# Attention queries and keys in three stacked copies: one rounded similarity pass of 96 rows in place of an exact one of 32

## The chip, the cores and the metric

The kernel runs on one core of a Trainium2 chip. The metric is the device time of one execution in microseconds (us). The kernel before was timed three times: 608.33, 611.28 and 616.86 us, median 611.28. One more execution was recorded by the hardware profiler; the rows below come from it.

Engines are named as in the profile: PE is TensorE (matmul), DVE is VectorE, ACT is ScalarE, POOL is GpSimd, SP is SyncE.

## The reference

An image batch of 16 x 16 x 16 x 192 goes through three layers with residuals: a blockwise DCT convolution, a gated attention over the 256 tokens of each image, and a mixture of 8 experts with two chosen per token. Only the attention's queries and keys matter here:

```python
def _L1_attn_ref(x, ln_w, ln_b, W_hidden, b_hidden, W_qk, b_qk, gamma, beta, W_out, b_out):
    normed = _layernorm(x, ln_w, ln_b)
    hg = jax.nn.silu(jnp.einsum('bsd,hd->bsh', normed, W_hidden) + b_hidden)
    v, gate = jnp.split(hg, 2, axis=-1)
    Z = jax.nn.silu(jnp.einsum('bsd,qd->bsq', normed, W_qk) + b_qk)   # 32 wide
    q = Z * gamma[0] + beta[0]
    k = Z * gamma[1] + beta[1]
    sim = jnp.einsum('bid,bjd->bij', q, k) / seq_len
    A = jnp.square(jax.nn.relu(sim))
    V = jnp.einsum('bij,bjd->bid', A, v) * gate
    out = jnp.einsum('bih,dh->bid', V, W_out) + b_out
    return out + x
```

## The kernel before, in words

The program has three stages, each a software pipeline written out by hand per engine: the convolution over 16 images (to about 120 us), the attention over 16 images (to about 300 us), and the experts' tiles. Every engine runs its own `attn_step(i)` for i from -1 to 16; in step i it works on image i, on the front of image i+1 and on the tail of image r = i-1. The order within an engine is the order of the code; engines meet through semaphores.

**Rounded and exact products.** A product with operands of type `fp32r` takes one pass of PE and rounds its operands. Where the kernel wants more precision it splits an operand into a rounded high part and the low rest and adds several such passes (`products`, five passes). A product with plain `f32` operands is exact and appears in the trace as two matmul rows for one call.

**PE, step i.** The v products of image i (10 matmuls of 392 columns), then the wait for `qk_done` and the similarity (`ps_sim`, two calls, one per half of the keys), the gate products (15 matmuls), the transposes of image i+1, `attend` (which waits for `attn_done` and `l1_done`), two small matmuls that count rows per expert, the z product of image i+1 (`z_product`, five matmuls), the output product. The next step's v products follow.

**ACT, step i.** silu of v, relu and square of the similarity, silu of the gate, the rounded copies of the next image's transposed rows (`nB_bias`, `n_hi`), silu of z into `zT` (L843), `normalise` for image i+2, tanh, and the expert rows of image r (`row_a`, L854).

**DVE, step i.** `finish_tokens(r)` (residual, moments, variance `u_var`), `logits_of_base`, `logits_of_tokens`, `choose(r)`, `low_parts(i+1)` (L940, L941), the gating product (L1253), `scale_tokens(r)` (L1189 to L1196), `query_key(i+1)` (L1063), `count(r)` (L1090 to L1092) and `place(r)` (L1100 to L1106). `scale_tokens` waits for POOL's power `u_pow`; `place` ends with the routing weights, on `weights_done`.

**POOL, step i.** `u_pow(r)` (L649, waits for DVE's `u_var`), the bias add on image i's residual (L654), two id updates (L661), the copy of `row_a` into `row_b` (L663, waits for ACT's row_a), then the wait for `weights_done` and `slots_done` of DVE's `place(r)`, and four indirect DMAs that scatter the rows to the experts' lists (L672). The next step's `u_pow` stands behind these four.

`query_key(i)` is two DVE instructions, each 32 partitions by 256:

```python
for n, dst in enumerate((qT, kT)):
    last = dve.tensor_scalar(dst[:, :], zT[:, :], gb_sb[:, n:n + 1], gb_sb[:, 2 + n:3 + n], ALU.mult, ALU.add)
last.then_inc(qk_done, 1)
```

In step 0 DVE also computes the layer-norm scales of the last four images, right behind `query_key(1)`; `logits_of_base(1)`, which gives `l1_done`, comes after them. `chain.link(ins)` makes DVE wait for its own instruction `ins` to finish before the next one.

Of the kernel before, what the change touches and what calls it, by code (L numbers as in the profile page):

```python
# [24 lines left out]
SEQ = SIDE * SIDE  # L25
P = 128
# [9 lines left out]
HID = 2 * D  # L36
QK = 32
EXPERTS, FF = 8, 768
FCHUNKS = FF // P
# [156 lines left out]
def build(nc, x, consts, w1, b1, ln_w, ln_b, w_hid, w_qk, b_hid, b_qk, b_i, gamma, beta, w_out, w_out_t, b_out, b_col, w_r,  # L196
# [8 lines left out]
    with ctx:  # L205
# [36 lines left out]

        w_qk_sb = sb("w_qk_sb", [P, 2, QK])
        w_qk_hi = sb("w_qk_hi", [P, 2, QK], f32r)
        w_qk_lo = sb("w_qk_lo", [P, 2, QK], f32r)
        w_out_sb = sb("w_out_sb", [P, HID // P, OUT_W])
# [3 lines left out]
        ln_sb = sb("ln_sb", [P, 2, 2])  # L250
        gb_sb = sb("gb_sb", [QK, 4])
        b_out_sb = sb("b_out_sb", [P, D])
# [14 lines left out]

        zT, qT, kT = (xc[0:QK, :, :, :].rearrange("p a t c -> p (a t c)")[:, n * SEQ:(n + 1) * SEQ] for n in range(3))
        hT = sb("hT", [P, 2, FCHUNKS, TWO])
# [102 lines left out]
        ps_nT = ps[:, 0, :].rearrange("p (k n) -> p k n", k=2)  # L372
        ps_z = ps[0:QK, 1, 0:SEQ]
        ps_sim = ps[:, 1, :].rearrange("p (t n) -> p t n", t=HALVES)
# [109 lines left out]
        def over_channels(ap):  # L484

            return ap.unsqueeze(1).unsqueeze(3).broadcast_to((P, HALVES, GROUPS, GC))

        def pad_lists(eng, experts, done):
# [216 lines left out]
        def _(act):  # L705
# [24 lines left out]
            def bias_high_parts():  # L730

                act.wait_ge(parts_done, 1)
                act.wait_ge(prep_ps, 1)
                hi, lo = slice(BIAS_HI, BIAS_HI + 1), slice(BIAS_LO, BIAS_LO + 1)
                act.activation(w_lo[hi, 1, 0:HID], ps_b_hid[hi, :], ACT.Copy)
                act.activation(b_hi[lo, 0:HID].bitcast(f32r), ps_b_hid[lo, :], ACT.Copy)
                act.activation(w_qk_lo[hi, 1, :], ps_b_qk[hi, :], ACT.Copy)
                act.activation(b_qk_hi[lo, :].bitcast(f32r), ps_b_qk[lo, :], ACT.Copy).then_inc(bias_hi_done, 1)
# [139 lines left out]
        def _(dve):  # L878
# [38 lines left out]
            def bias_low_parts():  # L917
# [4 lines left out]
                dve.tensor_tensor(w_lo[lo, 1, 0:HID], ps_b_hid[lo, :], b_hi[lo, 0:HID], ALU.subtract)  # L922
                dve.tensor_tensor(w_qk_lo[lo, 1, :], ps_b_qk[lo, :], b_qk_hi[lo, :], ALU.subtract)
                for row in (hi, lo):
# [135 lines left out]
            def query_key(i):  # L1060
                dve.wait_ge(z_done, i + 1)
                for n, dst in enumerate((qT, kT)):
                    last = dve.tensor_scalar(dst[:, :], zT[:, :], gb_sb[:, n:n + 1], gb_sb[:, 2 + n:3 + n],  # L1063
                                             ALU.mult, ALU.add)
                last.then_inc(qk_done, 1)
# [213 lines left out]
            dve.wait_ge(ld_rest, 16)  # L1279
            pipeline(dve, attn_step, **ATTN, chain=chain, per=8)  # L1280

# [39 lines left out]
        def _(pe):  # L1321
# [36 lines left out]
            def prepare():  # L1358
# [4 lines left out]
                folded_bias(ps_b_hid, hid_in[:, :, 0:HID], b_hid_sb[:, 0:HID])  # L1363
                folded_bias(ps_b_qk, w_qk_sb, b_qk_sb)
                for k in range(NKC):
# [73 lines left out]
            def z_product(i):  # L1439
                pe.wait_ge(nT_done, i + 1)  # L1440
                pe.wait_ge(nB_bias_done, i + 1)
                products(ps_z, w_qk_hi, w_qk_lo, slice(0, QK), False).then_inc(z_ps, 1)

# [53 lines left out]
            def attn_step(i):  # L1497
# [6 lines left out]
                if not absent(i):  # L1504

                    pe.wait_ge(qk_done, i + 1)
                    for t in range(HALVES):
                        last = mm(ps_sim[:, t, :], kT[:, t * P:(t + 1) * P], qT[:, :])
                    last.then_inc(sim_ps, 1)
# [121 lines left out]
```

## Time and profile before

| what | value |
|---|---|
| median of three runs | 611.28 us (608.33 to 616.86) |
| profiled execution, its own time | 614.02 us |
| its span, first to last instruction | 612.3 us |
| mean granted TensorE clock | 0.981 |
| PE busy | 578.3 us, 94% |
| DVE busy | 394.4 us, 64% |
| ACT busy | 332.1 us, 54% |
| POOL busy | 266.4 us, 44% |
| chain that ended last | PE 71%, DVE 10%, DMA 7%, issue 6% |

The shares are averages over the three stages. What matters is the attention stage, from about 120 to 300 us: there a view by stretches, a view in order of time and the chain that ended last are read together. In a row of the time view the first number is the start, the second the time from the first start to the last end of the instructions merged in the row (the count is at the end), and in brackets stands how long the engine sat idle before and what released it.

### The profile page before, as it was taken

Reading aid. Unit: us, or ns where it says so; the run is one execution under the profiler, and the core shown is the slowest. Engines: PE = TensorE matmul, PEld = TensorE weight load, DVE = VectorE, ACT = ScalarE, POOL = GpSimd, SP = SyncE. Lnnn points to the kernel's source line nnn. Section 1 sums busy time; section 2 is a strip of 40 time slices with the busy share of each in tenths; the row PEclk is TensorE's granted clock in tenths of the full one; section 3 lists DMA queues with packets and bytes.
Section 4 is the critical chain, followed back from the end, with each engine's and each line's share of the span. In section 5 each row is a group of like instructions: output and inputs, shape, how many; then the busy total and the mean of one; then the engine's idle time right before and its main releaser. Section 6 shows DMA issues by size and latency. Waiting matters only on the chain.

```text
span 612.3 us, 14343 instructions
## 1 busy us (share of the span) xinstructions
PE 578.3 (94%) x3844; PEld 544.6 (89%) x3845; DVE 394.4 (64%) x1516; ACT 332.1 (54%) x722; POOL 266.4 (44%) x314
## 2 busy tenths in 40 slices
PE   3999999898999999999898999999999999999992
PEld 2899888887888888888797999999999999999992
DVE  4568888757777767778876555555555555555650
ACT  1433233465666676666673555555555555556650
POOL 3313322103656565565565444444444444444432
PEclk9979999998999999999998999999999999999997
DMA  8980000310111111112224333333333333333221
GB/s 241 412 332 1 0 0 2 126 49 33 60 52 65 39 68 48 59 59 79 66 87 85 50 45 50 52 48 50 52 51 48 50 52 52 45 39 40 41 27 20
DMA packets 31832, 42.45 MB, mean 69 GB/s; under 512 B 4596, under 2 KB 27797, under 8 KB 31670
## 3 DMA queue, kind: packets, MB, share of 16 engines
q0 software_dynamic: 13488, 13.74, 14.4%
q1 hardware_dynamic: 18196, 28.16, 14.1%
q8 instruction: 15, 0.25, 0.2%
q14 instruction: 19, 0.16, 0.1%
q10 hardware_dynamic: 114, 0.15, 0.1%
HBM read 24.46 MB, written 17.57 MB: 69 GB/s over the span
## 4 chain that ended last, share of the span: by engine, by line
PE 71%; DVE 10%; DMA 7%; issue 6%; POOL 2%; DVEq 2%; ACT 1%; POOLq 0%; SPq 0%; ACTq 0%
PE ps L1326 68%; DMA out_rows<-const,y_id 6%; PE ps L1330 2%; PE ps L1331 2%; DMA X<-in_x 1%; DVEq L988 1%; POOL xn L639 1%; DVE newton L969 1%; POOL y_id L688 1%; DVE gsq L1005 1%; DVE mom L990 0%; DVE newton L1000 0%; DVE newton L1010 0%; DVE newton L994 0%; DVE newton L1009 0%
## 5 line engine op out<-in xcount | busy, mean ns | idle before, releaser
L806 ACT ACTIVATE hT<-ps,b_i_sb 128x256 f32<-128x256 f32 (+1 forms) x240 | 94.5, 448 | 114.3 <-PE ps L1326 114.2
L1326 PE MATMUL ps<-w_o_sb,hT 128*128 x852 | 146.9, 329 | 0.9 <-DVE const L1308 0.9
L1326 PEld LDWEIGHTS ps<-w_o_sb,hT 128*128 128x128 f32 x852 | 139.1, 192 | 1.5 <-issue 1.5
L692 POOL DMA_INDIRECT out_rows<-const,y_id x71 | 115.7, 1630 | 41.9 <-POOL y_id L688 29.4
L1326 PE MATMUL ps<-n_hi,we_hi 128*128 128x256 f32 (+1 forms) x468 | 124.7, 289 | 0.0
L1326 PE MATMUL ps<-n_hi,we_lo 128*128 128x256 f32 (+1 forms) x468 | 92.9, 280 | 0.0
L1211 DVE TENSOR_TENSOR we_lo<-we_all,we_hi 128x768 fp32r<-128x768 f32 x80 | 75.3, 982 | 23.1 <-issue 23.0
L1326 PEld LDWEIGHTS ps<-n_hi,we_hi 128*128 128x128 f32 x468 | 88.9, 190 | 0.0
L1326 PEld LDWEIGHTS ps<-n_hi,we_lo 128*128 128x128 f32 x468 | 71.6, 189 | 0.0
L1326 PE MATMUL ps<-nA_lo,we_hi 128*128 128x256 f32 (+1 forms) x234 | 65.6, 280 | 0.0
L787 ACT ACTIVATE we_hi<-we_all 128x768 fp32r x80 | 63.5, 849 | 3.4 <-DVE tile_expert L1149 2.6
L1308 DVE TENSOR_TENSOR const<-ps,b_o_sb 128x384 f32<-128x384 f32 (+1 forms) x40 | 20.5, 513 | 69.4 <-DMA out_rows<-const,y_id 56.3
L688 POOL TENSOR_TENSOR y_id<-y_row,no_offset 128x2 int32<-128x2 int32 (+1 forms) x40 | 9.8, 246 | 116.0 <-DVE const L1314 90.7
L1326 PE MATMUL ps<-attnT,hT 128*128 128x256 f32 x192 | 45.9, 391 | 2.3 <-issue 2.3
L1326 PEld LDWEIGHTS ps<-nA_lo,we_hi 128*128 128x128 f32 x234 | 44.3, 189 | 0.0
L672 POOL DMA_INDIRECT lists<-row_a,slots x32 | 32.8, 1026 | 22.8 <-POOL row_b L663 11.6
L639 POOL TENSOR_TENSOR xn<-xc,grs 128x384 f32<-128x384 f32 x16 | 13.8, 865 | 66.4 <-DVE grs L1011 54.5
L1326 PEld LDWEIGHTS ps<-attnT,hT 128*128 128x128 f32 x192 | 36.3, 196 | 7.0 <-issue 2.5
L1326 PE MATMUL ps<-w_out_sb,hT 128*128 128x200 f32 x192 | 36.6, 341 | 2.9 <-DVE hT L1253 2.6
L1326 PE MATMUL ps<-conv_only,coef 96*108 96x192 f32 x192 | 38.9, 356 | 0.4
L1326 PEld LDWEIGHTS ps<-w_out_sb,hT 128*128 128x128 f32 x192 | 31.8, 190 | 6.3 <-issue 3.9
L1221 DVE TENSOR_TENSOR nA_lo<-ps,n_hi 128x256 fp32r<-128x256 f32 (+1 forms) x39 | 15.3, 393 | 33.1 <-ACT n_hi L796 33.0
(238 smaller groups left out, 1154.1 us busy)
## 6 DMA issues: line engine op xcount, KB each, us to landing
we_all<-in_w_i SPq DMA_DIRECT2D x8, 768.0 KB, 13.7
conv_only<-lists SPq DMA_DIRECT2D x31, 194.0 KB, 2.8
w_o_sb<-in_w_o SPq DMA_DIRECT2D x8, 576.0 KB, 17.9
out_rows<-X SPq DMA_DIRECT2D x16, 192.0 KB
X<-in_x SPq DMA_DIRECT2D x1, 1536.0 KB, 11.7
out_rows<-const,y_id POOLq DMA_INDIRECT x71, 3.6
conv_only<-lists SPq DMA_DIRECT2D x9, 97.0 KB, 2.3
we_all<-in_w_hid SPq DMA_DIRECT2D x1, 776.0 KB, 8.0
```

Source lines behind the costliest of these rows:

```text
L639: pool.tensor_tensor(grouped(xn[:, :, :]), grouped(xc[:, odd, :, :]), over_channels(grs[:, :]), ALU.mult).then_inc(xn_done, 1)
L672: pool.indirect_dma_start(out=lists, out_offset=bass.IndirectOffsetOnAxis(ap=slots[:, c, t:t + 1], axis=0), in_=rows[:, t, :], in_offset=N ...
L688: pool.tensor_tensor(y_id[:, odd, 0:n], y_row[:, odd, 0:n], no_offset[:, 0:n], ALU.add).then_inc(id_done[odd], 1)
L692: pool.indirect_dma_start(out=out, out_offset=bass.IndirectOffsetOnAxis(ap=y_id[:, odd, t:t + 1], axis=0), in_=y_sb[:, odd, t, :], in_offs ...
L787: act.activation(we_hi[:, odd, here].unsqueeze(1), we_all[:, ds(e, 1), here], ACT.Copy).then_inc(we_hi_done, 1)
L806: last = act.activation(hT[:, odd, f, 0:n].unsqueeze(1), ps_h[:, b, c, 0:n].unsqueeze(1), ACT.Gelu, bias=b_i_sb[:, ds(e * FCHUNKS + f, 1)])
L1211: last = dve.tensor_tensor(we_lo[:, odd, here].unsqueeze(1), we_all[:, ds(e, 1), here], we_hi[:, odd, here].bitcast(f32).unsqueeze(1), ALU ...
L1221: dve.tensor_tensor(lo[:, 0:n * P], turned[:, 0, 0:n * P], hi[:, 0:n * P].bitcast(f32), ALU.subtract)
L1308: dve.tensor_tensor(here, ps_y[:, 0:n, :], b_o_sb[:, ds(e, 1), :].broadcast_to((P, n, D)), ALU.add).then_inc(y_read, 1)
L1326: return pe.matmul(dst, lhsT, rhs, start=start, stop=stop)
L1330: pe.transpose(dst[:, 0, here], rows[:, 0:KA], K("ident"))
L1331: return pe.transpose(dst[:, 1, here], rows[:, KA:WIDE], K("ident"))
```

## The change

z, the input of the queries and keys, is computed three times in one projection: the weights, gamma and beta are repeated three times over, so that z stands in 96 partitions. From it DVE makes `q_parts` and `k_parts`, 96 partitions by 256 of type `fp32r`: rounded values in all three blocks, and then in one block each (rows 64 to 95 for the queries, 32 to 63 for the keys) the exact value minus the rounded one. One rounded pass over 96 rows then sums high x high, high x low and low x high. For the subtraction the exact values of that block are computed as well, into `q_full` and `k_full`.

`query_key` has six instructions in place of two, with a wait of DVE for its own fourth before the fifth. The similarity is a rounded product in place of an exact one. The chain's count per step goes from 8 to 9.

```diff
+QK3 = 3 * QK
...
-        w_qk_sb = sb("w_qk_sb", [P, 2, QK])
-        w_qk_hi = sb("w_qk_hi", [P, 2, QK], f32r)
-        w_qk_lo = sb("w_qk_lo", [P, 2, QK], f32r)
+        w_qk_sb = sb("w_qk_sb", [P, 2, QK3])
+        w_qk_hi = sb("w_qk_hi", [P, 2, QK3], f32r)
+        w_qk_lo = sb("w_qk_lo", [P, 2, QK3], f32r)
...
-        gb_sb = sb("gb_sb", [QK, 4])
+        gb_sb = sb("gb_sb", [QK3, 4])
...
-        zT, qT, kT = (xc[0:QK, :, :, :].rearrange("p a t c -> p (a t c)")[:, n * SEQ:(n + 1) * SEQ] for n in range(3))
+        zT, q_full, k_full = (xc[0:QK3, :, :, :].rearrange("p a t c -> p (a t c)")[:, n * SEQ:(n + 1) * SEQ]
+                              for n in range(3))
+
+        q_parts = sb("q_parts", [QK3, SEQ], f32r)
+        k_parts = sb("k_parts", [QK3, SEQ], f32r)
...
-        ps_z = ps[0:QK, 1, 0:SEQ]
+        ps_z = ps[0:QK3, 1, 0:SEQ]
...
-                act.activation(w_qk_lo[hi, 1, :], ps_b_qk[hi, :], ACT.Copy)
+                act.activation(three_times(w_qk_lo[hi, 1, :]), one_for_three(ps_b_qk[hi, :]), ACT.Copy)
...
-                dve.tensor_tensor(w_qk_lo[lo, 1, :], ps_b_qk[lo, :], b_qk_hi[lo, :], ALU.subtract)
+                dve.tensor_tensor(three_times(w_qk_lo[lo, 1, :]), one_for_three(ps_b_qk[lo, :]),
+                                  one_for_three(b_qk_hi[lo, :]), ALU.subtract)
...
             def query_key(i):
                 dve.wait_ge(z_done, i + 1)
-                for n, dst in enumerate((qT, kT)):
-                    last = dve.tensor_scalar(dst[:, :], zT[:, :], gb_sb[:, n:n + 1], gb_sb[:, 2 + n:3 + n],
-                                             ALU.mult, ALU.add)
+                scales = [(gb_sb[:, n:n + 1], gb_sb[:, 2 + n:3 + n]) for n in range(2)]
+                rows = (slice(2 * QK, QK3), slice(QK, 2 * QK))
+                for full, here, (by, plus) in zip((q_full, k_full), rows, scales):
+                    dve.tensor_scalar(full[here, :], zT[here, :], by[here, :], plus[here, :], ALU.mult, ALU.add)
+                for parts, (by, plus) in zip((q_parts, k_parts), scales):
+                    last = dve.tensor_scalar(parts[:, :], zT[:, :], by, plus, ALU.mult, ALU.add)
+                chain.link(last)
+                for parts, full, here in zip((q_parts, k_parts), (q_full, k_full), rows):
+                    last = dve.tensor_tensor(parts[here, :], full[here, :], parts[here, :].bitcast(f32), ALU.subtract)
                 last.then_inc(qk_done, 1)
...
-            pipeline(dve, attn_step, **ATTN, chain=chain, per=8)
+            pipeline(dve, attn_step, **ATTN, chain=chain, per=9)
...
-                products(ps_z, w_qk_hi, w_qk_lo, slice(0, QK), False).then_inc(z_ps, 1)
+                products(ps_z, w_qk_hi, w_qk_lo, slice(0, QK3), False).then_inc(z_ps, 1)
...
-                        last = mm(ps_sim[:, t, :], kT[:, t * P:(t + 1) * P], qT[:, :])
+                        last = mm(ps_sim[:, t, :], k_parts[:, t * P:(t + 1) * P], q_parts[:, :])
...
-    w_qk = np.ascontiguousarray(two_parts(L1_attn_W_qk).swapaxes(0, 1))
+    w_qk = np.ascontiguousarray(np.tile(two_parts(L1_attn_W_qk).swapaxes(0, 1), (1, 1, 3)))
```

Two places show how the instructions stand. The first is DVE's stretch from `scale_tokens` to `place` in the attention loop, before (xc holds zT, qT and kT; list_at and slot belong to `count`):

```order
L1196 TENSOR_TENSOR diff<-diff,u_scale 128x2
L1063 TENSOR_SCALAR xc<-xc,gb_sb 32x256 [waits z_done]
L1063 TENSOR_SCALAR xc<-xc,gb_sb 32x256
L1090 TENSOR_TENSOR slot<-list_at,ps 128x8 [waits prefix_ps]
L1091 TENSOR_TENSOR slot<-slot,in_first 128x8 [waits dve_self]
L1092 TENSOR_TENSOR list_at<-list_at,ps 128x8
L1100 TENSOR_TENSOR picked<-chosen,slot 128x32 [waits prefix_read,ld_const]
L1102 TENSOR_REDUCE slots<-picked 128x4 [waits dve_self]
```

Two instructions make queries and keys, and `count` follows them. The same stretch in the changed kernel (xc now holds zT, q_full and k_full):

```order
L1216 TENSOR_TENSOR diff<-diff,u_scale 128x2
L1079 TENSOR_SCALAR xc<-xc,gb_sb 32x256 [waits z_done]
L1079 TENSOR_SCALAR xc<-xc,gb_sb 32x256
L1081 TENSOR_SCALAR q_parts<-xc,gb_sb 96x256
L1081 TENSOR_SCALAR k_parts<-xc,gb_sb 96x256
L1084 TENSOR_TENSOR q_parts<-xc,q_parts 32x256 [waits dve_self]
L1084 TENSOR_TENSOR k_parts<-xc,k_parts 32x256
L1110 TENSOR_TENSOR slot<-list_at,ps 128x8 [waits prefix_ps]
L1111 TENSOR_TENSOR slot<-slot,in_first 128x8 [waits dve_self]
L1112 TENSOR_TENSOR list_at<-list_at,ps 128x8
L1120 TENSOR_TENSOR picked<-chosen,slot 128x32 [waits prefix_read,ld_const]
L1122 TENSOR_REDUCE slots<-picked 128x4 [waits dve_self]
```

Four more instructions stand between `scale_tokens` and `count`, one of them with a wait for DVE itself; nothing else is moved.

The second place is PE's similarity, between the last v products (392 columns) and the first gate products, before:

```order
L1326 MATMUL ps<-w_lo,nB_bias 128x392
L1326 MATMUL ps<-w_lo,n_hi 128x392
L1326 MATMUL ps<-xc 128x256 x2
L1326 MATMUL ps<-n_hi,w_hi 128x256
L1326 MATMUL ps<-nA_lo,w_hi 128x256
```

The two calls read qT and kT in xc, exact products. The same place in the changed kernel:

```order
L1346 MATMUL ps<-w_lo,nB_bias 128x392
L1346 MATMUL ps<-w_lo,n_hi 128x392
L1346 MATMUL ps<-q_parts,k_parts 128x256 x2
L1346 MATMUL ps<-n_hi,w_hi 128x256
L1346 MATMUL ps<-nA_lo,w_hi 128x256
```

The two calls keep their place and their shape and read the rounded parts; the order of PE is otherwise the same.

## Rows read from the trace of the kernel before

**Rows 1.** Busy time per stretch: window, length, PE, PEld, DVE, ACT, POOL, PEclk, DMA.
```profile
114.00:120.00 6.00, 4.50 (x27) 4.26 (x28) 4.19 (x16) 3.36 (x8) 0.00 (x0) 1.00 0.41 115
...
138.00:144.00 6.00, 3.72 (x13) 2.92 (x11) 4.77 (x26) 2.25 (x5) 2.02 (x4) 0.78 0.09 33
...
190.00:201.00 11.00, 11.00 (x67) 9.72 (x67) 8.31 (x43) 7.62 (x18) 6.44 (x9) 1.00 0.15 54
```

**Rows 2.** The chain that ended last, in order of time: one step of the attention.
```profile
196.12 10.30 PE ps L1326 x60
```

**Rows 3.** Time view of POOL in the attention (columns as told above).
```profile
150.36 1.23 POOL L672 DMA_INDIRECT lists<-row_a,slots  x1 [1.13 <-issue]
...
193.16 1.06 POOL L672 DMA_INDIRECT lists<-row_a,slots  x1 [0.97 <-POOL row_b L663]
...
198.04 0.73 POOL L649 TENSOR_TENSOR u_pow<-u_var,minus_half 128x2 f32<-128x2 f32 x1
198.74 0.99 POOL L654 TENSOR_TENSOR X<-X,b_out_sb 128x384 f32 x1
...
203.88 1.05 POOL L672 DMA_INDIRECT lists<-row_a,slots  x1 [0.97 <-POOL row_b L663]
...
289.63 1.05 POOL L672 DMA_INDIRECT lists<-row_a,slots  x1 [1.00 <-DVE row_b L1106]
```

**Rows 4.** Time view of DVE in the same step.
```profile
197.31 0.42 DVE L940 TENSOR_TENSOR nA_lo<-ps,n_hi 128x256 fp32r<-128x256 f32 x1 [1.32 <-ACT n_hi L838]
197.75 0.43 DVE L941 TENSOR_TENSOR n_hi<-ps,n_hi 64x256 fp32r<-64x256 f32 x1
...
199.14 0.62 DVE L1189 TENSOR_TENSOR newton<-u_neg,u_pow 128x2 f32<-128x2 f32 x1
...
200.26 0.15 DVE L1196 TENSOR_TENSOR diff<-diff,u_scale 128x2 f32<-128x2 f32 x1
200.33 0.72 DVE L1063 TENSOR_SCALAR xc<-xc,gb_sb 32x256 f32<-32x256 f32 x2
200.98 0.14 DVE L1090 TENSOR_TENSOR slot<-list_at,ps 128x8 f32<-128x8 f32 x1
...
201.99 0.16 DVE L1106 TENSOR_SCALAR row_b<-tanh_d 128x2 f32<-128x2 f32 x1
```

**Rows 5.** Time view of PE: z product (two of five), similarity, first gate product.
```profile
198.60 0.28 PE L1326 MATMUL ps<-n_hi,w_qk_hi 128*32 128x256 f32 x1
198.72 0.28 PE L1326 MATMUL ps<-nA_lo,w_qk_hi 128*32 128x256 f32 x1
...
203.31 1.13 PE L1326 MATMUL ps<-xc 32*128 32x256 f32 x4
204.36 0.39 PE L1326 MATMUL ps<-n_hi,w_hi 128*128 128x256 f32 x1
```

**Rows 6.** Time view of DVE and POOL in the last image, where POOL waits for DVE.
```profile
314.05 0.50 POOL L663 COPY row_b<-row_a 128x384 f32<-128x384 f32 x1 [1.64 <-ACT row_a L854]
314.05 0.54 DVE L1100 TENSOR_TENSOR picked<-chosen,slot 128x32 f32<-128x32 f32 x1
...
314.80 0.16 DVE L1106 TENSOR_SCALAR row_b<-tanh_d 128x2 f32<-128x2 f32 x1
315.88 1.05 POOL L672 DMA_INDIRECT lists<-row_a,slots  x1 [1.33 <-DVE row_b L1106]
```

**Rows 7.** One line, shortest, median and longest duration in ns: DVE L1314, per-partition scalars.
```profile
L1314 DVE TENSOR_SCALAR const<-const,meta x71: 310/320/322, 316.0 to 602.6; 128x192 f32<-128x192 f32 x71
```

**Rows 8.** Time view of DVE and PE in images 0 and 1.
```profile
123.01 0.72 DVE L1063 TENSOR_SCALAR xc<-xc,gb_sb 32x256 f32<-32x256 f32 x2
123.87 1.13 PE L1326 MATMUL ps<-xc 32*128 32x256 f32 x4
...
131.06 0.72 DVE L1063 TENSOR_SCALAR xc<-xc,gb_sb 32x256 f32<-32x256 f32 x2 [0.45 <-ACT xc L843]
...
140.50 4.52 PE L1326 MATMUL ps<-attnT,hT 128*128 128x256 f32 x12 [2.28 <-issue]
```

More of the change, by code:

```diff
@@ L486, in over_channels, with three_times, one_for_three @@
             return ap.unsqueeze(1).unsqueeze(3).broadcast_to((P, HALVES, GROUPS, GC))
+        def three_times(ap):
+            return ap.rearrange("p (n c) -> p n c", n=3)
+        def one_for_three(ap):
+            return ap.unsqueeze(1).broadcast_to((1, 3, QK))
         def pad_lists(eng, experts, done):
@@ L1363, in prepare @@
                 folded_bias(ps_b_hid, hid_in[:, :, 0:HID], b_hid_sb[:, 0:HID])
-                folded_bias(ps_b_qk, w_qk_sb, b_qk_sb)
+                folded_bias(ps_b_qk, w_qk_sb[:, :, 0:QK], b_qk_sb)
                 for k in range(NKC):
@@ L1612 @@
         "b_qk": np.asarray(L1_attn_b_qk).reshape(1, -1), "b_i": np.ascontiguousarray(b_i.T),
-        "gamma": np.ascontiguousarray(np.asarray(L1_attn_gamma).T),
-        "beta": np.ascontiguousarray(np.asarray(L1_attn_beta).T),
+        "gamma": np.ascontiguousarray(np.tile(np.asarray(L1_attn_gamma).T, (3, 1))),
+        "beta": np.ascontiguousarray(np.tile(np.asarray(L1_attn_beta).T, (3, 1))),
         "w_out": packed(L1_attn_W_out, P), "w_out_t": packed(np.asarray(L1_attn_W_out).T, KC),
```

## The prediction

> **What bounds the kernel now.** I read the busy time per stretch first. In the attention's steady state PE is busy in 11.00 of 11.00 us, DVE in 8.31, ACT in 7.62, POOL in 6.44, at a granted clock of 1.00 [rows 1]. The chain that ended last agrees: through ten steps it shows PE pieces of 10.30 us [rows 2], and nothing else of weight. So this stage is bound by PE, with a step of 203.88 - 193.16 = 10.72 us by POOL's first scatter [rows 3]; the 13 steps from 150.36 to 289.63 give 139.27 / 13 = 10.71.
>
> The change shortens work on PE and lengthens work on DVE, so the next question is how much room DVE has. Busy time says 2.7 us in 11, but DVE does not work alone: there is a ring through DVE and POOL. POOL's four scatters of one image wait for the weights that DVE's `place` writes; POOL's `u_pow` of the next image stands behind these four; DVE's `scale_tokens` waits for `u_pow`; behind it come `query_key`, `count`, `place`, and with these the next scatters. The time view gives each link:
>
> - first scatter to `u_pow`: 198.04 - 193.16 = 4.88 [rows 3];
> - `u_pow` start to the end of DVE's first Newton step: 199.14 + 0.62 = 199.76, so 1.72 [rows 3, 4]. That step is stretched until POOL's bias add ends, 198.74 + 0.99 = 199.73;
> - Newton end to `query_key`: 200.33 - 199.76 = 0.57 [rows 4];
> - `query_key` to `count`: 200.98 - 200.33 = 0.65 [rows 4];
> - `count` to the end of `place`: 201.99 + 0.16 - 200.98 = 1.17 [rows 4];
> - end of `place` to the first scatter, where POOL really waits for it: 315.88 - (314.80 + 0.16) = 0.92 [rows 6].
>
> The ring is 9.91 us long, against a step of 10.72. It has only 0.81 us of room, and in the row of 203.88 POOL's bracket names the copy of row_b and not DVE as the last to come [rows 3], as it must where the ring is slack.
>
> **The change part by part.**
>
> The similarity on PE. Two exact calls are four matmul rows and last from 203.31 to the first gate product at 204.36, so 1.05 us [rows 5]. Rounded passes of 256 columns start 0.12 apart (198.60, 198.72); two take 0.24. PE gains 0.8 us per image, and a step bound by PE would be 9.92.
>
> The z product. Five passes of 256 columns stay five passes of 256 columns; only the stationary side is 96 wide and not 32. I take nothing for it; whatever it were, PE's idle time below would hide it. ACT's silu of z works on 96 partitions and 256 elements as before: nothing.
>
> `query_key` on DVE. Before, the two instructions take 0.72 together and `count` starts 0.65 after the first [rows 4]: one starts about 0.325 after the other and lasts 0.395. Now there are six. What their order costs is bounded from both sides.
>
> The lower end: all overlap as the two do now. The fourth starts at 0.975 and ends at 1.37; DVE's wait for itself adds about 0.04; two subtractions of 256 elements follow 0.34 apart; `count` starts at 2.09. That is 2.09 - 0.65 = 1.44 more.
>
> The upper end: instructions that change the block of partitions do not overlap. L941 works on partitions 64 to 127, L940 before it on all, and it starts at 197.75, 0.02 after the 0.42 of L940 have ended (197.31 + 0.42), while the pair of `query_key` overlaps by 0.07 [rows 4]. The six work from partitions 64, 32, 0, 0, 64, 32, and `count` from 0. Then the first starts 0.10 later than now, the next two at 0.41 and 0.82, the fourth at 1.15, ending at 1.54; the subtractions of 0.42 each run from 1.58 and 2.02 to 2.44; `count` starts at 2.46. That is 0.10 + 2.46 - 0.65 = 1.91 more.
>
> The Trainium skill has a rule for this, in "VectorE: DVE Perf Modes", section "Two Vector instructions with no wait between them": an instruction whose input or output starts in another quadrant of 32 partitions than the one before it starts only when every earlier one has finished. By it the added time is the 1.91, without it the 1.44. L941's row agrees with it.
>
> On top of this a subtraction with both inputs in SBUF can meet POOL's copy of row_b, which lasts 0.50. In the last image such an instruction (`picked`) and the copy both start at 314.05; it takes 0.54 and ends 0.04 after the copy [rows 6]. The Newton step in rows 4 does the same with the bias add. So this costs between 0 and 0.5; I take 0.1, since the copy can start only after tanh and row_a, which follow `scale_tokens`, and so should be nearly over when the subtractions come. The scaling instructions take per-partition scalars, as L1314 does, and L1314 is never stretched in 71 cases, though POOL issues its indirect DMAs in the same stage [rows 7]; for them I take no wait. The skill's page "SBUF — State Buffer", section "Who interferes with whom", says the same: a VectorE instruction with two SBUF inputs and a GpSimd one that reads SBUF exclude each other for their whole length.
>
> I take 1.91 + 0.1 = 2.0 per image (ends 1.4 and 2.4). Behind the last subtraction stand `count` and `place`, on which POOL's scatters wait, so all of it lies in the ring: 9.91 + 2.0 = 11.9 us per step (11.3 to 12.3). That is longer than the PE step of 9.92, so PE's gain is idle time (DVE's own work, 8.31 x 10.72 / 11 + 2.0 = 10.1, also stays below it), and the step grows by 11.9 - 10.7 = 1.2 us (0.6 to 1.6). From the first scatter to the fourteenth there are 13 such steps: 15.6 us (8 to 21).
>
> Before the steady state. In image 0, `query_key` starts at 123.01 and PE's similarity follows at 123.87 [rows 8]. The queries are now ready at 123.01 + 2.44 = 125.45, PE starts about 1.7 later and saves 0.8: +0.9. In image 1, `query_key` at 131.06 stands ahead of the layer-norm scales, on which `l1_done` and with it PE's `attend` at 140.50 wait, idle 2.28 [rows 8]: 1.8 more (no earlier instruction to wait out). In image 2 the ring closes for the first time; its first scatter at 150.36 is not bound by DVE yet, and of the 2.0 I count 0.6. Together 3.3 (2.2 to 3.9).
>
> After the fourteenth scatter no `query_key` is left; the last images' chain runs through DVE's weight parts and POOL, shifted as a whole. The experts' stage is the same code. The wider weights cost three ACT and three DVE instructions with up to 64 more elements each per part, 0.1 us or less each by the 0.42 for 256 [rows 4], in the first two conv steps: 0.2, at most 0.5.
>
> Sum: 15.6 + 3.3 + 0.2 = 19.1 us. Against the profiled execution's 614.02 (1.7 of it outside the span) that is 633.1; this execution lies 2.7 above the median of 611.28, so the forecast for a median is 611.28 + 19.1, rounded to 630. The ends give 622 and 637.
>
> **The rivals.**
>
> *The six overlap after all* (0.13). The block of partitions does not matter to instructions that read SBUF only, and the copy is not met. For: L941 reads PSUM too, so its row is not quite the same case. Against: in the same rows every pair that stays on one block of partitions overlaps, and only L941 does not. The ring is 9.91 + 1.44 = 11.35, 0.63 more per step: 8.2, with 2.2 at the start and 0.2, 622.
>
> *PE stays the bound and the kernel gets faster* (0.06). The ring would have to have room that I don't see: the 0.92 from `place` to the scatter would have to pass while DVE still works, as a fixed time of POOL's after its copy and not after the last release. For: behind the copy POOL takes 0.97 as well [rows 3]. Against: in rows 6 the scatter keeps 0.92 from DVE's end while the copy had ended at 314.55, 1.33 before. It decides if the ring with the new `query_key` stays under 9.92; then 14 images save 0.8: 611.28 - 11 = 600.
>
> *PE's clock falls* (0.11). With 2.0 us of idle time per step of 11.9 PE might be granted less. For: after the idle 2.28 the clock is 0.78 in 138 to 144 [rows 1, 8]. Against: from 114 to 120 PE is busy in only 4.50 of 6.00 us, at a clock of 1.00 [rows 1]. PE's 9.92 would pass 11.9 at a clock below 0.83; at 0.78 it is 12.7, 0.8 more per step, about 11 in 13 steps: 641.
>
> **How the numbers follow.** The forecast, the ring with about 2.0 us more in it, has 0.70; its own range is 624 to 637. The point is its 630. The rivals have 0.13 (622), 0.06 (600) and 0.11 (641). The range from 618 to 640 holds nearly all of the forecast, the first rival and part of the clock's, and leaves out the faster case. Two per cent, about what a measurement of this kernel can tell from no change, is 12.2 us: 599.1 and 623.5. Slower than that: 0.67 of the forecast, the clock's 0.11, and 0.03 of the first rival, 0.81. Within: 0.03, 0.10 and half of the faster case's, 0.16. Faster: 0.03.
>
> **What would show it.** The interval between first scatters should be 11.9 and the bracket of the first one should name DVE's row_b of `place`, not POOL's copy. From the first `query_key` instruction to `count` it should be about 2.5, with no overlap between the instructions that start on different partitions, and one of the subtractions may be stretched by POOL's copy. PE should sit idle ahead of the similarity, released by DVE, and be busy in about 10 of 12 us. Two similarity rows per image should stand 0.12 apart. The forecast is wrong if PE stays busy throughout with steps near 9.9, if `query_key` takes under 2.0, or if POOL's scatters are released by its copy as before.

## The result, and the profile after

The changed kernel takes 636.19 us (median of four runs, 635.88 to 637.79) against 610.53 for the kernel before in the same comparison (four runs, 608.33 to 616.86). The ratio is 1.0403, interval 1.0356 to 1.0451: slower by 4%. The profiled execution of the changed kernel took 635.88 us with a span of 634.2, the one before 614.02 with 612.3; the spans differ by 21.9.

Busy time per stretch, after, in the order window, length, PE, PEld, DVE, ACT, POOL, PEclk, DMA; this answers to [rows 1]:

```profile
138.00:144.00 6.00, 3.00 (x7) 2.49 (x8) 4.82 (x28) 0.07 (x1) 2.00 (x4) 0.56 0.09 33
...
202.00:214.00 12.00, 10.16 (x62) 9.17 (x62) 10.31 (x47) 7.31 (x17) 6.43 (x9) 1.00 0.16 56
```

In the steady state PE now idles 1.84 of 12 us, at a clock of 1.00, and DVE does 10.31; but DVE isn't full either. No engine is the bound; a chain is. POOL's time view shows it:

```profile
152.19 1.23 POOL L685 DMA_INDIRECT lists<-row_a,slots  x1 [1.83 <-issue]
...
209.39 0.51 POOL L676 COPY row_b<-row_a 128x384 f32<-128x384 f32 x1 [1.87 <-ACT row_a L867]
212.73 1.05 POOL L685 DMA_INDIRECT lists<-row_a,slots  x1 [2.84 <-DVE row_b L1126]
...
217.60 0.74 POOL L662 TENSOR_TENSOR u_pow<-u_var,minus_half 128x2 f32<-128x2 f32 x1
...
224.79 1.06 POOL L685 DMA_INDIRECT lists<-row_a,slots  x1 [2.84 <-DVE row_b L1126]
...
285.03 1.05 POOL L685 DMA_INDIRECT lists<-row_a,slots  x1 [2.73 <-DVE row_b L1126]
...
310.87 1.05 POOL L685 DMA_INDIRECT lists<-row_a,slots  x1 [2.73 <-DVE row_b L1126]
```

The step is 224.79 - 212.73 = 12.06 (before 10.72 in [rows 3]). The bracket of the first scatter has changed: it was 0.97 behind POOL's copy, now it is 2.84, and the releaser is DVE's row_b. POOL sits with its copy done and waits for `place`.

DVE in the same step, the answer to [rows 4]:

```profile
207.96 0.82 DVE L1079 TENSOR_SCALAR xc<-xc,gb_sb 32x256 f32<-32x256 f32 x2
208.80 0.41 DVE L1081 TENSOR_SCALAR q_parts<-xc,gb_sb 96x256 fp32r<-96x256 f32 x1
209.13 0.40 DVE L1081 TENSOR_SCALAR k_parts<-xc,gb_sb 96x256 fp32r<-96x256 f32 x1
209.57 0.60 DVE L1084 TENSOR_TENSOR q_parts<-xc,q_parts 32x256 fp32r<-32x256 f32 x1
210.18 0.41 DVE L1084 TENSOR_TENSOR k_parts<-xc,k_parts 32x256 fp32r<-32x256 f32 x1
210.63 0.16 DVE L1110 TENSOR_TENSOR slot<-list_at,ps 128x8 f32<-128x8 f32 x1
...
211.67 0.16 DVE L1126 TENSOR_SCALAR row_b<-tanh_d 128x2 f32<-128x2 f32 x1
...
213.36 0.39 DVE L1181 TENSOR_SCALAR u_neg<-mom 128x2 f32<-128x2 f32 x1
...
214.02 0.37 DVE L1193 SCALAR_TENSOR_TENSOR from_base<-ps,a_scale,sums 128x8 f32<-128x8 f32 x2 [0.26 <-DVE both_parts L1184]
...
218.44 0.89 DVE L1209 TENSOR_TENSOR newton<-u_neg,u_pow 128x2 f32<-128x2 f32 x1 [0.65 <-POOL u_pow L662]
...
220.02 0.82 DVE L1079 TENSOR_SCALAR xc<-xc,gb_sb 32x256 f32<-32x256 f32 x2
```

Follow the ring from the scatter at 212.73: `u_pow` 4.87 later; end of the Newton step at 219.33, 1.73 later; next `query_key` at 220.02, 0.69; `query_key` to `count`, 210.63 - 207.96 = 2.67; to the end of `place`, 211.83, 1.20; to the scatter, 0.90. The sum is 12.06, which is the step.

PE, the answer to [rows 5] and [rows 8] (image 1, a steady step, and step 13, behind DVE's first counting of tiles):

```profile
141.00 5.09 PE L1346 MATMUL ps<-attnT,hT 128*128 128x256 f32 x12 [4.96 <-issue]
...
210.65 0.50 PE L1346 MATMUL ps<-q_parts,k_parts 96*128 96x256 f32 x2 [0.41 <-DVE k_parts L1084]
210.99 0.28 PE L1346 MATMUL ps<-n_hi,w_hi 128*128 128x256 f32 x1
...
214.49 1.75 PE L1346 MATMUL ps<-attnT,hT 128*128 128x256 f32 x7 [1.12 <-issue]
...
287.93 4.47 PE L1346 MATMUL ps<-attnT,hT 128*128 128x256 f32 x12 [2.15 <-issue]
```

The similarity has shrunk as the change intends: the first gate product follows 0.34 behind it, where it was 1.05. But PE waits 0.41 for the queries and then 1.12 ahead of `attend`.

Where the 21.9 us of span went, by POOL's first scatters:

| stretch | before | after | difference |
|---|---|---|---|
| to image 0's `query_key` | 123.01 | 120.63 | -2.4 |
| from there to the first scatter | 27.35 | 31.56 | +4.2 |
| next 11 steps | 118.03 | 132.84 | +14.8 |
| two steps after these | 21.24 | 25.84 | +4.6 |
| 14th to 15th first scatter | 15.46 | 14.22 | -1.2 |
| from the 15th to the end | 307.2 | 309.1 | +1.9 |

The first line lies ahead of what the change touches in the attention. In the twelve profiled executions here image 0's `query_key` starts between 117.55 and 123.01, latest in the one of the kernel before; its granted clock in 30 to 60 us is 0.85, that of the changed kernel 0.95.

### The profile page after: what moved, and what is told of

It is laid out like the page before. It is cut to its first block, busy times and chain, and to the rows that moved or that the text cites. A ratio compares the mean times of both kernels' runs of the same rounds, so it can differ in the third digit from the quotient of the medians.

```text
span 634.2 us, 14353 instructions
## 1 busy us (share of the span) xinstructions
PE 569.7 (90%) x3812; PEld 540.7 (85%) x3813; DVE 426.6 (67%) x1580; ACT 333.8 (53%) x722; POOL 273.2 (43%) x314
## 4 chain that ended last, share of the span: by engine, by line
PE 46%; DVE 2%; issue 1%; DMA 1%; POOLq 0%; DVEq 0%; ACT 0%; ACTq 0%; POOL 0%
PE ps L1346 44%; PE ps L1350 1%; PE ps L1351 1%; DMA out_rows<-const,y_id 1%; POOLq L206 0%; DVE const L1334 0%; DVE hT L1273 0%; DVE we_lo L1231 0%; DVE meta L1244 0%; DVE const L1328 0%; DVE over L1138 0%; DVE nA_lo L1241 0%; DVE n_tiles L1140 0%; DVE n_hi L1242 0%; ACTq L796 0%
## 5 line engine op out<-in xcount | busy, mean ns | idle before, releaser
L705 POOL DMA_INDIRECT out_rows<-const,y_id x71 | 123.2, 1736 | 41.9 <-POOL y_id L701 29.4
L1231 DVE TENSOR_TENSOR we_lo<-we_all,we_hi 128x768 fp32r<-128x768 f32 x80 | 73.4, 959 | 22.1 <-issue 20.6
L1346 PE MATMUL ps<-attnT,hT 128*128 128x256 f32 x192 | 49.0, 409 | 21.9 <-issue 21.9
L1346 PEld LDWEIGHTS ps<-attnT,hT 128*128 128x128 f32 x192 | 37.7, 203 | 30.0 <-issue 24.9
L1346 PE MATMUL ps<-w_out_sb,hT 128*128 128x200 f32 x192 | 38.2, 351 | 4.1 <-DVE hT L1273 4.0
L1346 PEld LDWEIGHTS ps<-w_out_sb,hT 128*128 128x128 f32 x192 | 33.5, 197 | 5.8 <-issue 4.3
L1346 PE MATMUL ps<-conv_only,coef 96*108 96x192 f32 x192 | 37.4, 346 | 0.4
```

Source lines behind the costliest of these rows:

```text
L705: pool.indirect_dma_start(out=out, out_offset=bass.IndirectOffsetOnAxis(ap=y_id[:, odd, t:t + 1], axis=0), in_=y_sb[:, odd, t, :], in_offs ...
L1231: last = dve.tensor_tensor(we_lo[:, odd, here].unsqueeze(1), we_all[:, ds(e, 1), here], we_hi[:, odd, here].bitcast(f32).unsqueeze(1), ALU ...
L1346: return pe.matmul(dst, lhsT, rhs, start=start, stop=stop)
```

## The experiments

The kernels are named by what was done. Ratios are against the kernel before, run beside them (611.48, 611.45 or 610.96 us). A step is the mean interval of POOL's first scatters over eight or nine steady steps.

**Late `place` alone.** The kernel before, similarity and queries untouched, with four instructions of the change's shapes behind `qk_done` whose output nobody reads:

```diff
                 last.then_inc(qk_done, 1)
...
+                for n, here in enumerate(rows):
+                    last = dve.tensor_scalar(full_any[here, :], z_any[here, :], ...)
+                chain.link(last)
+                for here in rows:
+                    dve.tensor_tensor(parts_any[here, :], full_any[here, :], z_any[here, :], ALU.subtract)
```

> The kernel before with its exact similarity; qk_done is given by the second of the two query instructions as before, and behind them DVE runs four more that nobody reads (two scalings of 32 rows from partitions 64 and 32, DVE's wait for itself, two subtractions of 32 rows). The ring theory (POOL's scatters wait for DVE's place, which now comes about 2.0 us later): step between first scatters 12.0, POOL's first scatter released by DVE's row_b, about 634 us. The rival (the changed kernel is slower because PE's similarity waits for its queries): the queries are on time here, so steps stay at 10.7 and the time at 611.

Measured: 630.28 us, ratio 1.031 (1.0276 to 1.0345), step 12.02. In the time views of POOL and PE:

```profile
207.33 1.13 PE L1337 MATMUL ps<-xc 32*128 32x256 f32 x4
...
209.83 1.05 POOL L676 DMA_INDIRECT lists<-row_a,slots  x1 [2.82 <-DVE row_b L1117]
```

PE's similarity starts without a wait, and the step is still 12.02, with the same bracket on the scatter. So delaying `count` and `place` is by itself enough for the step of the changed kernel; late queries aren't needed for it. The other 6 us of the changed kernel are not in this one: of the 5.4 by which its span is shorter, 2.4 lie ahead of the first scatter and 1.8 in the two steps behind the steady ones.

**Rounded values only.** The changed kernel without its exact values and subtractions. All three blocks then hold rounded values and high x high is summed three times, so the output is not only less exact, as the expectation has it, but another one; the kernel serves for its time:

```diff
-                for full, here, (by, plus) in zip((q_full, k_full), rows, scales):
-                    dve.tensor_scalar(full[here, :], zT[here, :], by[here, :], plus[here, :], ALU.mult, ALU.add)
...
-                chain.link(last)
-                for parts, full, here in zip((q_parts, k_parts), (q_full, k_full), rows):
-                    last = dve.tensor_tensor(parts[here, :], full[here, :], parts[here, :].bitcast(f32), ALU.subtract)
...
```

> The changed kernel without the low parts: the exact values and the two subtractions are left out, so query_key is two instructions of 96 rows as short as before (the output is less exact). Ring theory: the ring is 9.9 again and PE's step is 10.7 less 0.8, so steps of 9.9 to 10.0, about 601 us (597 to 605). Rival (the wider z product or the rounded similarity cost something): steps at 10.7 or more, 611 or more.

Measured: 604.41 us, ratio 0.9893 (0.9844 to 0.9942), step 10.19. This is 1% less than the kernel before, and the interval lies wholly below 1: it is the gain on PE that the change could have had. Other tokens may go to other experts here, but from the last first scatter to the end the profile has 296.7 us, against 296.4 before, so the gain isn't from there. The run shows the ring once more:

```profile
204.60 0.51 POOL L676 COPY row_b<-row_a 128x384 f32<-128x384 f32 x1 [1.81 <-ACT row_a L867]
204.70 0.44 DVE L1121 TENSOR_SCALAR row_a<-tanh_d 128x2 f32<-128x2 f32 x1
206.11 1.06 POOL L685 DMA_INDIRECT lists<-row_a,slots  x1 [1.00 <-DVE row_b L1121]
```

With a faster PE the scatter is released by DVE and no longer by the copy. `place`'s first weight takes 0.44 where it takes 0.16 elsewhere, and ends 0.03 after POOL's copy; the second starts at 205.05. The old ring of 9.91 plus about 0.27 is the step.

**No copy on POOL.** ACT writes row_b too:

```diff
-                    pool.tensor_copy(row_b[:, :, DATA:ROW], row_a[:, :, DATA:ROW]).then_inc(row_b_done, 1)
...
-                    pool.wait_ge(row_b_done, r + 1)
...
-                    for t in range(HALVES):
...
+                    for rows in (row_a, row_b):
+                        for t in range(HALVES):
...
```

> The changed kernel without POOL's copy of the expert rows: ACT writes row_b itself, by two more instructions behind row_a. In the changed kernel the first subtraction of query_key takes 0.60 and ends 0.27 after POOL's copy, the second 0.41. Theory (the subtraction waits for the copy's end): it takes 0.42, the six instructions and count come closer by 0.18, the step falls from 12.07 to 11.89 and the time by 13 x 0.18 = 2.3 to about 634. Rival (the 0.60 is DVE's wait for its own fourth instruction): the subtraction stays at 0.60 and the step at 12.07, 636.

Measured: 632.33 us, ratio 1.0348 (1.024 to 1.0456), step 11.84.

**One block of partitions.** The same, and the exact values made over all 96 partitions:

```diff
-                for full, here, (by, plus) in zip((q_full, k_full), rows, scales):
-                    dve.tensor_scalar(full[here, :], zT[here, :], by[here, :], plus[here, :], ALU.mult, ALU.add)
+                for full, (by, plus) in zip((q_full, k_full), scales):
+                    dve.tensor_scalar(full[:, :], zT[:, :], by, plus, ALU.mult, ALU.add)
```

> The kernel without POOL's copy, and the exact values made over all 96 partitions from partition 0, not over 32 partitions from 64 and from 32: the first four instructions of query_key now start on one partition. Theory (an instruction that starts on another block of partitions waits for the end of the one before): the four start 0.33 apart, where the changed kernel shows 0.41, 0.42 and 0.33, and the first of them need not wait out scale_tokens (0.1); so about 0.28 less from scale_tokens to count, a step of about 11.6 and a time of about 630. Rival (no such wait; the 0.41 is the length of an instruction that works on 32 partitions): 96 partitions change nothing, step as without the copy alone, about 11.9, 634.

Measured: 628.6 us, ratio 1.0257 (1.0169 to 1.0345), step 11.53. DVE without the copy:

```profile
204.16 0.15 DVE L1215 TENSOR_TENSOR diff<-diff,u_scale 128x2 f32<-128x2 f32 x1
204.35 0.82 DVE L1078 TENSOR_SCALAR xc<-xc,gb_sb 32x256 f32<-32x256 f32 x2
...
205.95 0.42 DVE L1083 TENSOR_TENSOR q_parts<-xc,q_parts 32x256 fp32r<-32x256 f32 x1
```

and with one block of partitions:

```profile
204.52 0.15 DVE L1215 TENSOR_TENSOR diff<-diff,u_scale 128x2 f32<-128x2 f32 x1
204.59 0.73 DVE L1078 TENSOR_SCALAR xc<-xc,gb_sb 96x256 f32<-96x256 f32 x2
...
206.01 0.42 DVE L1083 TENSOR_TENSOR q_parts<-xc,q_parts 32x256 fp32r<-32x256 f32 x1
```

Without POOL's copy the first subtraction falls from 0.60 to 0.42: the 0.18 was the copy. With one block the first instruction follows `diff` by 0.07 and not 0.19, and from it to the subtraction 1.42 pass and not 1.60, though each instruction now works on three times the partitions. So the step loses 0.12 + 0.18 = 0.30 (measured 11.84 - 11.53 = 0.31). An instruction that changes the block of partitions waits for the one before, which is what the Trainium skill states in "VectorE: DVE Perf Modes", section "Two Vector instructions with no wait between them"; here the wait costs 0.08 to 0.12 a time.

**`place` first.** The changed kernel with `count` and `place` ahead of `query_key`:

```diff
+                if not absent(r):
+                    count(r)
+                    place(r)
                 if not absent(i + 1):
                     query_key(i + 1)
...
-                if not absent(r):
-                    count(r)
-                    place(r)
```

> The changed kernel with count and place ahead of query_key in DVE's order; nothing else. Ring theory: the six instructions are out of the ring, which is 9.3; DVE's own order of work (newton, count and place, six query instructions, residual to choose, low parts, gating) is then the longest at about 10.5 a step; about 614 us (608 to 619). Rival (late queries hold PE): the queries come 1.2 us later still, so the steps stay at 12 or grow to 13, 636 or more.

Measured: 628.05 us, ratio 1.027 (1.0221 to 1.0319), step 11.26. A miss. PE, ACT, DVE and POOL in one step:

```profile
201.48 2.83 PE L1346 MATMUL ps<-attnT,hT 128*128 128x256 f32 x12
...
205.33 1.64 ACT L729 ACTIVATE normed<-X,n_bias,n_scale 128x192 f32 x4
206.87 0.19 ACT L862 ACTIVATE tanh_d<-diff 128x2 f32<-128x2 f32 x1
...
207.09 0.17 DVE L1126 TENSOR_SCALAR row_a<-tanh_d 128x2 f32<-128x2 f32 x1 [0.57 <-ACT tanh_d L862]
...
208.07 0.50 POOL L676 COPY row_b<-row_a 128x384 f32<-128x384 f32 x1 [2.90 <-ACT row_a L867]
208.20 0.52 DVE L1081 TENSOR_SCALAR q_parts<-xc,gb_sb 96x256 fp32r<-96x256 f32 x1
```

`place` now meets tanh, which stands on ACT behind `normalise`, which stands behind the silu of z. In the kernel before this wait was covered by `query_key` itself. A new loop closes: PE's `attend` and z, ACT's silu, `normalise` and tanh, DVE's `place` and `query_key`, and the next `attend`, at 212.74, one step of 11.26 later. `low_parts` is no link of it: it ends at 203.73, and z starts at 204.20, right behind `attend` and the two small counting matmuls.

**`place` first, exact values on ACT.** As above, and ACT computes the two exact values behind `row_a`; the subtractions wait for them:

```diff
+                if not absent(i + 1):
+                    act.wait_ge(z_done, i + 2)
+                    for n, (full, at) in enumerate(((q_full, 2 * QK), (k_full, QK))):
+                        here = slice(at, at + QK)
+                        last = act.activation(full[here, :], zT[here, :], ACT.Identity, ...)
+                    last.then_inc(exact_done, 1)
...
-                for full, here, (by, plus) in zip((q_full, k_full), rows, scales):
-                    dve.tensor_scalar(full[here, :], zT[here, :], by[here, :], plus[here, :], ALU.mult, ALU.add)
...
+                dve.wait_ge(exact_done, i + 1)
```

> The changed kernel with place ahead of query_key and the two exact values computed by ACT behind row_a in place of DVE; same result. Ring theory: DVE's order of work is 0.85 shorter than in e2_place_first, about 9.7, PE 9.9 and the ring through row_a and its copy about 10.0; steps of 10.0, about 602 us (598 to 608), faster than the kernel before. Rival (ACT's extra 0.7 us delays silu of v or tanh): steps of 10.5 or more, 609 or more.

Measured: 634.92 us, ratio 1.0367 (1.033 to 1.0403), step 11.38. The second miss, of the same cause: behind `normalise`, tanh and `row_a` the exact values are late.

```profile
202.49 0.42 DVE L1091 TENSOR_TENSOR q_parts<-xc,q_parts 32x256 fp32r<-32x256 f32 x1 [1.31 <-ACT xc L875]
```

The 0.82 saved on DVE comes back as a wait of 1.31.

**`normalise` ahead of z.** `place` first, and ACT runs `normalise(i+2)` before the silu of z, so that tanh isn't behind it:

```diff
+                if not absent(i + 2):
+                    normalise(i + 2)
                 if not absent(i + 1):
                     act.wait_ge(z_ps, i + 2)
                     act.activation(zT[:, :], ps_z, ACT.Silu).then_inc(z_done, 1)
-                if not absent(i + 2):
-                    normalise(i + 2)
```

> The changed kernel with count and place ahead of query_key on DVE, and with ACT's normalise of image i+2 ahead of its silu of z, so that tanh and row_a no longer stand behind normalise. Theory (with place first the step of 11.26 is DVE's own order, 10.5 of work and 0.57 of waiting for tanh): the wait is gone, the step is about 10.7, DVE is busy all but 0.3 of it, and the time is about 7 below that of place first alone, 621. Rival 1 (the ring through row_a and the copy binds, 11.24): row_a starts 1.3 earlier, so the step falls as well, but with POOL's copy and not DVE's row_b ahead of the first scatter, and DVE idle more. Rival 2 (normalise ahead of z delays z, and with it queries and similarity): step stays near 11.2, 628.

Measured: 631.81 us, ratio 1.0302 (1.0215 to 1.0388), step 12.03. The wait for tanh is gone, yet the step has grown. DVE and POOL:

```profile
204.34 0.73 POOL L662 TENSOR_TENSOR u_pow<-u_var,minus_half 128x2 f32<-128x2 f32 x1
204.44 1.63 DVE L1105 TENSOR_TENSOR in_first<-chosen 128x8 f32<-128x8 f32 x1
205.04 0.99 POOL L667 TENSOR_TENSOR X<-X,b_out_sb 128x384 f32 x1
```

`in_first` adds two tiles of 128x8 and takes 0.15 in the changed kernel. Here it takes 1.63 (the median of its 16 executions is 1.62) and ends 0.04 after POOL's bias add.

**The same, with a later bias add.** One wait more on POOL:

```diff
+                    if not absent(i + 1):
+                        wait(pool, nT_done, i + 2)
                     wait_alone(pool, sum_done, i + 1, ld_const)
                     pool.tensor_tensor(whole, whole, b_out_sb[:, :]...
```

> The kernel with normalise ahead of z and place first, with one wait more: POOL's bias add waits until DVE's low_parts of the next image is done. In the kernel without this wait DVE's in_first (two inputs in SBUF, 0.15 elsewhere) takes 1.63 and ends with POOL's bias add in every step, and the step is 12.03 where 10.7 was expected. Theory (that instruction waits for the POOL instructions that began just after it was due): in_first takes 0.15 to 0.9 (u_pow alone may still meet it), the step falls by 0.8 to 1.4 to 10.6 to 11.2, the time to 614 to 621. Rival (the 1.63 is a wait for something else that the profile does not show, such as the semaphore behind in_row): it stays at 1.63 and the step at 12.0, 632.

Measured: 620.17 us, ratio 1.0154 (1.0102 to 1.0207), step 10.71.

```profile
210.61 0.73 POOL L662 TENSOR_TENSOR u_pow<-u_var,minus_half 128x2 f32<-128x2 f32 x1
210.72 0.15 DVE L1107 TENSOR_TENSOR in_first<-chosen 128x8 f32<-128x8 f32 x1
...
211.85 1.01 POOL L669 TENSOR_TENSOR X<-X,b_out_sb 128x384 f32 x1 [0.50 <-DVE n_hi L957]
```

A wait added to POOL makes the step 1.3 shorter: `in_first` is back at 0.15. That settles the 1.63, and with it the step of 10.7 that was expected of the kernel without this wait is there.

**Both moves and the exact values on ACT.** `normalise` ahead of z, `place` first, the exact values on ACT as above:

> As the kernel with normalise ahead of z and place ahead of query_key, and the two instructions for the exact values of query_key moved from DVE to ACT, behind row_a. Theory (DVE's work binds once place comes first): 0.8 less on DVE, so the step is 0.5 to 0.8 below that kernel's, 10.0 to 10.3, now near PE's own 9.9 and POOL's ring; the time is about 611 (604 to 618), level with the kernel before. Rival (the subtractions wait for ACT's exact values, as in the earlier kernel of this kind, 1.3 per step): the step stays at 10.7 or above, 621 or more.

Measured: 615.65 us, ratio 1.004 (0.9996 to 1.0084), step 10.39. With the order mended the steady state is faster than the kernel before (10.71), and PE is busy in 11.78 of 12 us (the mean of six stretches), so it is nearly bound by PE again. DVE waits 0.88 for ACT's values, and POOL's first scatter follows the copy by 0.97. What is left is at the ends of the stage: the first scatter is at 150.22, and the two steps after the steady ones take 12.51 and 12.79.

**Three mends of the ends.** On top of that, three moves, told in the expectation:

> The kernel with place first, normalise ahead of z and the exact values on ACT (615.7), with three further moves: for the first two steps normalise stays behind z; the layer-norm scales of the last four images stand behind logits_of_base(1), so that PE's attend of image 1 need not wait for them; the counting of tiles for images 12 and 13 stands between the rounded values and the subtractions, where DVE waits 0.88 for ACT. Theory (the rest of the loss is at the two ends of the stage and these waits make it): PE's 4.96 of idle time ahead of attend of image 1 falls below 2, the two last steps fall from 12.5 and 12.8 to about 11.3, first scatter about 4 earlier, time 609 (604 to 613), level with the kernel before or 1% faster. Rival (the ends are bound by the same ring through ACT's row_a and POOL's copy): no more than 2 us gained, 614 to 616.

Measured: 618.74 us, ratio 1.0138 (1.0094 to 1.0183), step 10.39. A miss, 3 us above the kernel without the three moves: the first scatter is at 151.86 and the two steps take 12.11 and 12.87. The wait ahead of `attend` of image 1 is gone, and another has come in its place:

```profile
146.41 0.19 PE L1355 MATMUL ps<-in_row,before_bf 128*128 128x8 bf16 x1 [5.55 <-DVE in_row L1118]
```

The scales now stand ahead of `choose`, whose `in_row` PE waits for. No version with the exact values was found that beats the kernel before.

## Why the prediction was right

**The ring as the bound: right, and shown.** Forecast were a step of 11.9 and a scatter released by DVE's row_b; the profile has 12.06 and that releaser. Of the 0.15 that is missing, 0.08 is POOL's copy (below); the rest are hundredths in the other links. That a late `place` causes it and not the late queries is shown by the first experiment, and that PE alone would have gained by the second: 604 against the 600 of the rival in which PE stays the bound.

**The cost of `query_key`.** The six take the course forecast: the first two, which change the block of partitions, take 0.84 from the first start to that of `q_parts`, 0.42 each, and `q_parts` and `k_parts` start 0.33 apart. The rival in which they overlap is refuted by the trace, and the one-block kernel shows the price, 0.30 per step. The subtraction does meet POOL's copy: 0.18, in every steady step, where 0.1 was taken. The copy had begun 0.18 ahead of the subtraction, so 0.33 of it were left and not the 0.5 of the upper end.

**PE's idle time: there, but elsewhere.** Forecast was that PE waits ahead of the similarity. It waits 0.41 there and 1.12 ahead of `attend`. The step "PE sits idle ahead of the similarity" looked only at who needs `k_parts`. But `finish_tokens` and `logits_of_base` stand behind `place`, so `l1_done`, on which `attend` waits, is as late as `place`: `from_base`, which gives it, ends at 214.39, and `attend` starts at 214.49. Another part of this lateness isn't in the sum, in every second step: `u_neg` at 213.36 takes 0.39, beside POOL's scatter of 212.73, where it takes 0.17 in the steps between, and with `place` first. The sum was not hurt, since `l1_done` isn't in the ring.

**The start: 4.2 and not 3.3.** The prediction has a term for each of three images, 0.9, 1.8 and 0.6. DVE's `query_key` of images 0 and 1 (120.63 in the table, 123.01 and 131.06 in [rows 8]) and PE's `attend` of image 1 part them:

```profile
129.71 0.82 DVE L1079 TENSOR_SCALAR xc<-xc,gb_sb 32x256 f32<-32x256 f32 x2 [0.28 <-ACT xc L856]
```

- From the first `query_key` to the second: 9.08 after, 8.05 before, 1.0 more where 0.9 was taken.
- From there to `attend`: 11.29 after, 9.44 before, 1.85 more where 1.8 was taken. PE's idle time there rose by 2.7, from 2.28 to 4.96, because PE comes to `attend` only 0.2 later than before, counted from the first `query_key`, while `attend` starts 2.9 later.
- From `attend` to the first scatter: 11.19 after, 9.86 before, 1.3 more where 0.6 was taken. This is the mis-sized term. 0.57 of it is `attend` itself, 5.09 for 4.52, with a granted clock in 138 to 144 of 0.56, where it was 0.78. The rest is 0.76, so image 2 has more of the ring in it than was counted: the first scatter starts 1.07 behind the end of `place` and 1.83 behind that of the copy, where before it was 1.13 behind the copy.

**The two steps behind the steady ones: 4.6 and not 2.4.** "13 such steps" was the error: in the last two DVE also counts tiles. Here the clock of the prediction's third rival falls, in one step. DVE ends step 12 with the counting (five instructions from 284.03), and the tokens of step 13 follow:

```profile
284.03 0.16 DVE L1135 TENSOR_TENSOR n_list<-list_at,const 128x8 f32<-128x8 f32 x1
...
285.29 0.55 DVE L1177 TENSOR_TENSOR X<-X,ps 128x384 f32<-128x384 f32 x1
...
290.80 0.69 DVE L1273 TENSOR_TENSOR hT<-ps,hT 128x512 f32<-128x512 f32 x1 [0.54 <-PE ps L1346]
292.44 0.42 DVE L1273 TENSOR_TENSOR hT<-ps,hT 128x256 f32<-128x256 f32 x1 [0.94 <-PE ps L1346]
```

and the busy times per stretch (columns as above) show the clock behind PE's idle stretch:

```profile
288.00:290.00 2.00, 2.00 (x7) 1.69 (x8) 1.81 (x13) 0.00 (x0) 1.67 (x3) 0.74 0.22 76
290.00:292.00 2.00, 2.00 (x6) 1.50 (x5) 0.95 (x2) 0.00 (x0) 1.89 (x4) 0.50 0.14 50
```

The counting delays the tokens by 1.26, PE idles 2.15, then the granted clock is 0.74 and 0.50 in the two stretches (0.50 is the lower of its two levels, 1.2 of 2.4 GHz), and `attend` takes 4.47, where it takes 2.83 one step earlier. DVE, in the ring, now waits for PE, 0.54 and 0.94. Before, the same counting cost nothing: the ring had room, and PE did not idle ahead of that `attend`. That the counting starts this was not tried alone: the kernel that moved it moved two other things as well.

**The end: 1.9 that nothing was forecast for.** One product holds 1.7 of it. The last image's output product starts 5.6 ahead of the 15th first scatter in both kernels, and PE's first products for the experts stand behind it. Before:

```profile
299.48 2.27 PE L1326 MATMUL ps<-w_out_sb,hT 128*128 128x200 f32 x12 [2.62 <-DVE hT L1253]
```

and after, with the busy times of a stretch in it:

```profile
319.47 3.95 PE L1346 MATMUL ps<-w_out_sb,hT 128*128 128x200 f32 x12 [3.66 <-DVE hT L1273]
...
320.00:322.00 2.00, 2.00 (x7) 2.00 (x7) 1.96 (x6) 1.08 (x3) 0.64 (x1) 0.50 0.45 112
```

It takes 1.68 longer, behind a longer idle stretch and at a granted clock of 0.50, where the kernel before has 1.00 in 300 to 302. The 16th first scatter then follows the 15th in 12.46 and not 10.79.

So the clock fell, though not in the steady steps, as the rival has it: there it is 1.00. It fell at three single places, where the products took 0.57, 1.64 and 1.68 longer. That the clock is the cause there is read from the traces; no run tried it alone.

**The sum.** Forecast were 19.1 us (15.6 in the 13 steps, 3.3 ahead of them, 0.2 for weights), measured 21.9 in the profiled pair: 19.4, 4.2, and -1.7 in the lines of the table that nothing was forecast for. Per steady step the forecast was 1.2, measured 14.8 / 11 = 1.35. The 21.9 come nearer to the forecast than they should, by the luck of the -2.4 in the table's first line: from image 0's `query_key` on the pair lies 24.3 apart, where 18.9 was forecast. The medians lie 25.7 apart, since the profiled execution before lies 3.5 above its median and the one after 0.3 below. The range held 636, near the upper end of the sum's own 637, though the terms at the ends of the stage had been put too low or left out.

## What to carry to other kernels

An engine that is busy all the time is the bound only while every ring of waits through the other engines is shorter; add the links of such a ring before shortening the busy engine, and compare the work added with the ring's room (here 0.81 against 2.0), not with an engine's idle time (2.7). Work put on an engine delays all that stands behind it in its order, so put it behind the instruction that others wait for, and then look at what that instruction itself waits for (here tanh, behind `normalise`). A kernel of balanced rings answers to small shifts: one reorder met a collision that cost 1.3 per step, and one more wait took it away.

## What the runs showed of the hardware that was not expected

- `in_first`, 0.15 long, took 1.63 with POOL's bias add of 0.99. It lasts until that ends, but it began 0.60 before the bias add by the records. `u_pow`, which ran at that time, isn't the cause: in the kernel with the later bias add it starts 0.11 ahead of `in_first` as well, and `in_first` takes 0.15. So, unless POOL's recorded start is late by that much, an instruction of POOL that is queued right behind another can hold up DVE before it starts. Who excludes whom agrees with the Trainium skill, "SBUF — State Buffer", section "Who interferes with whom": two inputs in SBUF on DVE, and a GpSimd instruction that reads SBUF. When the hold begins, no run here settles.
- DVE instructions with one input in SBUF and fixed scalars are held up too: `place`'s weight by the copy (0.44 for 0.16, rounded values only), `u_neg` during a scatter (0.39 for 0.17, in the changed kernel). The scaling with per-partition scalars hardly is: with `place` first, `q_parts` takes 0.52 beside the copy of 208.07, and 0.41 elsewhere.
- A granted clock of 0.50 behind 2.15 us of PE's idle time at 287.93 and behind 3.66 at 319.47, where the steady steps run at 1.00 with PE idle in 1.84 of 12 us, 0.41 and 1.12 of it in two pieces. In the kernel before, the clock stays at 1.00 behind 2.62 of idle time at 299.48. What parts these cases, no run here settles.
